# Output projections: the low halves of the scaled rows, subtracted by GpSimd behind each batch's bias instead of by VectorE

## The reference, cut to what matters

```python
    # layer 0: the heads are concatenated, no weight and no bias
    x = x + tanh(g_xattn[0]) * attention0(...)
    # layer 1 (and layer 6 in the same form)
    out = einsum('bhnm,bhmd->bhnd', softmax(scores), v).transpose(0, 2, 1, 3).reshape(b, n, c)
    x = x + tanh(g_xattn[1]) * (out @ Wproj + bproj)
    # layer 7: four quarters of the tokens, each with its own width m = 256, 128, 64, 32
    out = einsum('bnm,om->bno', attn_out[:, sl, :m], o_w[:m, :m]) + o_b[:m]
    x = x + tanh(g_ffn[3]) * (pad(out) + layernormed_x[:, sl, :])
```

## Time and profile before

| what | value |
|---|---|
| median of 3 runs | 6405.42 us (6404.94 to 6412.81) |
| the profiled execution: its own time | 6402.19 us |
| the profiled execution: its span | 6400.5 us |
| busy in the span | PE 4673.8 us (73%), DVE 3955.7 (62%), ACT 2808.6 (44%), POOL 2015.4 (31%) |
| granted TensorE clock, mean | 0.847 |
| the four output projections | 51 to 55 us each of the 6400.5 |

### The profile page before, as it was taken

The page is one execution under the profiler, slowest core; times in us unless marked ns, Lnnn a source line. Parts: engine busy times, 40 slices in busy tenths (PEclk is TensorE's granted clock), DMA queues, the critical chain, the costliest instruction groups (busy, mean ns, idle before and its releaser), DMA issues. The chain is left out here.

```text
span 6400.5 us, 101248 instructions
## 1 busy us (share of the span) xinstructions
PE 4673.8 (73%) x24710; PEld 2852.0 (45%) x24710; DVE 3955.7 (62%) x8261; ACT 2808.6 (44%) x5978; POOL 2015.4 (31%) x3020
## 2 busy tenths in 40 slices
PE   7455666482778972897675767797677887995897
PEld 4113333231453331786233645585555763334533
DVE  6335555547537875444477966558866556885465
ACT  2235554124225752322453556535466323771353
POOL 0114442000007640221353554124542214542242
PEclk9558999796898986998777979999889998996797
DMA  4999885000043320210551232102321115322433
GB/s 158 293 342 196 199 202 157 15 0 0 0 167 103 91 77 4 75 40 27 139 152 61 102 116 72 31 6 83 139 72 42 29 60 169 95 73 85 158 123 102
DMA packets 317804, 648.40 MB, mean 101 GB/s; under 512 B 73170, under 2 KB 128115, under 8 KB 317384
## 3 DMA queue, kind: packets, MB, share of 16 engines
q1 hardware_dynamic: 245912, 450.68, 21.8%
q0 software_dynamic: 71488, 193.32, 12.3%
HBM read 373.99 MB, written 238.70 MB: 96 GB/s over the span
## 5 line engine op out<-in xcount | busy, mean ns | idle before, releaser
L1115 DVE TENSOR_REDUCE t_nmax<-t_aps 128x2 f32<-128x1024 f32 x700 | 838.2, 1221 | 276.2 <-PE t_aps L1037 270.9
L1222 ACT ACTIVATE t_expT<-t_bps 128x512 f32<-128x512 f32 x1290 | 700.9, 599 | 283.8 <-PE t_bps L1056 233.4
L1056 PE MATMUL t_bps<-t_Q,t_K 51*128 51x512 f32 (+2 forms) x1290 | 525.9, 468 | 59.2 <-ACT t_expT L1222 43.4
L1037 PE MATMUL t_aps<-t_K,t_Q 49*128 49x512 f32 (+2 forms) x1400 | 464.6, 460 | 64.7 <-DMA t_K<-k_halves 30.0
L1056 PEld LDWEIGHTS t_bps<-t_Q,t_K 51*128 51x128 f32 (+2 forms) x1290 | 228.4, 189 | 526.2 <-ACT t_expT L1222 372.9
L2474 DVE TENSOR_TENSOR f_hl<-f_h,f_hh 128x512 fp32r<-128x512 f32 x192 | 203.7, 1061 | 411.2 <-ACT f_hh L2399 411.2
L1083 PE MATMUL t_ops<-t_expT,t_V 128*17 128x512 f32 (+1 forms) x2560 | 414.0, 615 | 0.4 <-ACT t_expT L1222 0.4
L3880 ACT ACTIVATE t_relsb<-t_relsb,t_nmax 128x128 f32<-128x128 f32 (+3 forms) x515 | 277.9, 559 | 272.1 <-DVE t_nmax L3853 268.7
L3814 PE MATMUL t_tps<-ident,t_relsb 128*128 128x128 f32 x1280 | 242.8, 292 | 165.5 <-ACT t_expT L3702 154.7
L2763 POOL TENSOR_TENSOR a_crossed<-a_qsb,a_tab 128x256 f32<-128x256 f32 x272 | 268.2, 1007 | 300.2 <-ACT a_qsb L2710 269.8
L1156 POOL DMA_DIRECT2D t_Q<-q_halves x525 | 270.9, 518 | 155.5 <-POOLq L78 86.2
(11 more groups left out here) (431 smaller groups left out, 12509.3 us busy)
## 6 DMA issues: line engine op xcount, KB each, us to landing
rel<-r_out SPq DMA_DIRECT2D x128, 640.0 KB, 5.4
t_relsb<-rel SPq DMA_DIRECT2D x128, 640.0 KB, 6.2
t_Q<-q_halves POOLq DMA_DIRECT2D x420, 64.0 KB, 2.5
t_K<-k_halves POOLq DMA_DIRECT2D x420, 64.0 KB, 2.6
k_halves<-a_parts SPq DMA_DIRECT2D x48, 512.0 KB
q_halves<-a_parts SPq DMA_DIRECT2D x48, 512.0 KB, 5.6
o_xT<-attended SPq DMA_DIRECT2D x32, 512.0 KB, 4.2
f_R<-combine SPq DMA_DIRECT2D x128, 128.0 KB, 2.9
```

What stands on the lines that cost most here:

```text
L1037: last = nc.tensor.matmul(aps[:, (t * PPG + i) % 2, x, :], operand(Qr, KA, p, h, slice(t * P, (t + 1) * P)), operand(Kr, KA, p, h, slice(0 ...
L1056: nc.tensor.matmul(bps[:, slot_of(kb, j), :], operand(Kr, KB, p, h, slice(kb * P, (kb + 1) * P)), operand(Qr, KB, p, h, slice(0, S)), star ...
L1115: nc.vector.tensor_reduce(nmax[:, g, t, i * HPT:(i + 1) * HPT], aps[:, (t * PPG + i) % 2], AX.X, ALU.max, negate=True).then_inc(s["maxed"], 1)
L1222: nc.scalar.activation(expT[:, kb % RING, j, :], bps[:, slot_of(kb, j), :], ACT.Exp).then_inc(s["expo"], 1 + (PAD if end else 0))
```

## The change

`lower(b)` moves from VectorE's program into GpSimd's. There it stands behind the bias of the same batch; in o0, which has no bias, the eight of them stand alone. What it computes and what it waits for (`xh` of its batch, and `y` of the batch two before, which frees the `xl` buffer) is unchanged.

```diff
+                def lower(b):
+                    pool.wait_ge(s["xh"], (b + 1) * KO)
+                    wait(pool, "y", (b - 1) * 2)
+                    nc.gpsimd.tensor_tensor(fast(xl[:, b % 2]), xn[:, b % 2], xh[:, b % 2], ALU.subtract).then_inc(s["xl"], 1)
+
                 if bias is None:
+                    for b in range(NB):
+                        lower(b)
                     return
...
                     last.then_inc(s["biased"], 1)
+                    lower(b)
...
-                def lower(b):
-                    dve.wait_ge(s["xh"], (b + 1) * KO)
-                    wait(dve, "y", (b - 1) * 2)
-                    nc.vector.tensor_tensor(fast(xl[:, b % 2]), xn[:, b % 2], xh[:, b % 2], ALU.subtract).then_inc(s["xl"], 1)
...
                 scale(0)
-                lower(0)
                 for b in range(NB):
                     if b + 1 < NB:
                         scale(b + 1)
                     if b:
                         add(b - 1)
-                    if b + 1 < NB:
-                        lower(b + 1)
                 add(NB - 1)
```

## The result

The changed kernel took 6413.27 us (median of 20 runs, 6391.84 to 6430.65), the kernel before, on the same chips, 6399.10 (20 runs, 6382.13 to 6413.23). The ratio is 1.0023, with a 95% interval from 1.0013 to 1.0034: slower by 14.2 us, and by 8 to 22 us with the interval, so whether it is more or less than 0.2% stays open. The profiled execution of the change took 6418.53 us, with a span of 6416.9.

The account below looks back on a forecast made before the run. VectorE sets the steady pace by a hair over TensorE, which waits on the line from spread to `xl`. The terms 1.7 + 2.4 + 4.6 + 4.1 = 12.8 us on the 6405.42 median gave 6418.2, range 6411 to 6432, the forecast's own 6415 to 6421.

Parts of the forecast that it names:

- The subtraction's price: All four output projections: one subtraction takes 2.36 us alone on GpSimd against 1.22 on VectorE, 1.14 more.
- o0: the line: o0: spread to project through GpSimd's subtraction takes 5.00 us, two batches at least 7.94; project(7) 1.7 us later.
- o1 and o3: GpSimd the bound: o1, o3: bias plus subtraction cost GpSimd 4.65 us a batch against TensorE's 3.59; +2.4 us and +4.6 us.
- aren't held up either: o1, o3: with both on GpSimd, neither its biases nor the subtraction are held up by the other engine.
- The clock rival: o1, o3, o0: TensorE's idling drops its clock from 2.4 to 1.2 GHz; 6428, or 6438 if throughout; chance 0.18.
- such a collision: First batches: a GpSimd bias holds up VectorE's subtraction, 3.44 us in place of 1.22 at 5799.29; mostly covered.
- my 10 us: Clock low in half of the twelve batches, 6 times 1.65 us, put on top of the forecast: 6428.
- The ring: o7: scale to `xh` 1.97, GpSimd's subtraction 2.36, then the held-up L1547 1.21: 5.54 us a batch.
- +4.1: o7: L1547 waits for nearly the whole GpSimd subtraction each batch; phase ends at 6389.4 against 6385.3, +4.1 us.
- The rival in which L1547 isn't held up: o7 keeps its time, the sum is 8.7 us, 6414; chance 0.11.
- The sum: All four phases: 1.7 + 2.4 + 4.6 + 4.1 = 12.8 us, with unknown lags 12 to 15.
- The relief of VectorE: Rival, not slower: VectorE's batch falls from 3.66 to 2.44 us, 0.4 gained per phase, 6403; chance 0.07 with similar outcomes.

Follow-up runs that it names:

- the repeated profiles: Both kernels run and profiled again, unedited: the change 6416.54 us against 6399.31, ratio 1.0024; the kernel before against itself 0.9994.
- Run 3: Changed kernel with GpSimd's subtraction in two halves, each begun once its half of `xh` is there; one execution, 6396.62 us.
- Run 2: Changed kernel with the bias of o1 and o3 left out, so GpSimd only subtracts there; one execution, 6417.01 us.
- Run 7: Kernel before, with the bias fetched earlier and o7's adds of `inner` for batches 3 to 7 made in the head; 6392.12 us, ratio 0.9992.
- run 4: Kernel before, VectorE's subtraction kept, plus a second copy on GpSimd that nobody reads and scale waits for; 6450.74 us in one run.
- run 6: Changed kernel with o7's add of `inner` (L1551) put ahead of the same batch's four other adds; 6411.20 us, ratio to before 1.0025.
- run 1: Changed kernel with o7's eight adds of `inner` (L1551) made ahead of the stretch in which GpSimd subtracts; one execution, 6427.33 us.

## Why the prediction was right, step by step

**The subtraction's price** held: 2.36 us forecast from one row of another phase, 2.36 in the median of 32.

**o0: the line.** Predicted was a pair of batches in 7.94 us and project(7) later by 1.7. TensorE's timeline of the change:

```profile
1118.34 0.73 PE L1451 MATMUL o_rps<-o_rows,o_sel 32*128 32x512 f32 x2
1118.99 0.39 PE L1461 MATMUL o_yps<-o_Wh,o_xh 128*128 128x256 f32 x1
...
1121.93 0.72 PE L1451 MATMUL o_rps<-o_rows,o_sel 32*128 32x512 f32 x2
...
1123.40 0.39 PE L1461 MATMUL o_yps<-o_Wh,o_xh 128*128 128x256 f32 x1 [0.74 <-POOL o_xl L1493]
```

From the start of a spread to the next project it is 0.65 in one batch, then 1.47, and starts of project are 4.41 and 3.61 apart, 8.02 a pair. The start of project(7) behind spread(2) was 24.8 us, against 22.78: +2.0 (+1.75 between the repeated profiles). Run 3 shortened the line and the pair with it.

**o1 and o3: GpSimd the bound.** Predicted 4.65 a batch. GpSimd's and TensorE's timelines in o1:

```profile
2404.04 2.37 POOL L1493 TENSOR_TENSOR o_xl<-o_xn,o_xh 128x1024 fp32r<-128x1024 f32 x1
2406.38 2.39 POOL L1511 TENSOR_TENSOR stream<-stream,o_B 128x1024 f32<-128x1024 f32 x1
2408.74 2.37 POOL L1493 TENSOR_TENSOR o_xl<-o_xn,o_xh 128x1024 fp32r<-128x1024 f32 x1
```

```profile
2411.16 0.39 PE L1461 MATMUL o_yps<-o_Wh,o_xh 128*128 128x256 f32 x1 [1.03 <-POOL o_xl L1493]
...
2415.85 0.38 PE L1461 MATMUL o_yps<-o_Wh,o_xh 128*128 128x256 f32 x1 [1.03 <-POOL o_xl L1493]
```

GpSimd is back to back, 4.70 from one subtraction to the next, TensorE idles 1.03 us and starts a project each 4.69. Project(7) behind spread(2): 28.69 against 25.84 in o1, +2.85 (+2.4 predicted, +2.4 in the second pair), and 28.54 against 23.84 in o3, +4.7 (+4.6 predicted, +4.9 in the second). Of the 0.45 that the prediction lacked in o1, about half lies ahead of project(2) and half in 4.69 a batch in place of 4.65. Run 2 took the bias away and the bound went. That GpSimd's biases "aren't held up either" held too: 2.339 to 2.399 us in all 16.

**The clock rival did not come.** Windows of TensorE in o1 of the change:

```profile
2412.00:2416.00 4.00, 2.97 (x23) 1.00 0.00 0
2420.00:2424.00 4.00, 3.00 (x24) 1.00 0.00 0
```

The engine idled 1.03 us of each 4.69 at a granted clock of 1.00, that is 2.4 GHz, from 3 us behind spread(2) to the last project, in o1 and in o3 and in both profiles of the change; even the 1.67 us before project(7) did not change it. The clock of the kernel before, in both of its profiles, fell once in o1 (0.61 in the earlier trace rows), and in the change this fall is gone: that is part of why o1 lost 2.85 and o3 4.7. Run 7 corrects the prediction here. It said that most of such a collision is covered, yet the one in o1 had cost 3.0 us with the fall of the clock behind it; the sum stands all the same, since it is taken from the measured start of project(7). The late fall in run 3 cost some 1.5 us, and with idles of 1.7 to 2.0 us in every batch (run 4) the clock fell again and again. So the rival is not excluded for another execution; where it came it cost less than my 10 us. The granted clock of the span, 0.844, doesn't tell: the phases are a thirtieth of it.

**o7: right mechanism, a term too large.** VectorE's and GpSimd's timelines in the change:

```profile
6366.06 1.09 DVE L1542 SCALAR_TENSOR_TENSOR stream<-o_yps,gate,stream 128x256 f32<-128x256 f32 x4
6367.18 3.12 DVE L1551 SCALAR_TENSOR_TENSOR stream<-inner,gate,stream 128x1024 f32<-128x1024 f32 x1
6370.22 1.27 DVE L1531 TENSOR_TENSOR o_xn<-o_xT,o_rps 128x512 f32<-128x512 f32 x2
```

```profile
6366.87 2.34 POOL L1493 TENSOR_TENSOR o_xl<-o_xn,o_xh 128x1024 fp32r<-128x1024 f32 x1 [0.77 <-ACT o_xh L1480]
...
6372.22 2.34 POOL L1493 TENSOR_TENSOR o_xl<-o_xn,o_xh 128x1024 fp32r<-128x1024 f32 x1 [0.43 <-ACT o_xh L1480]
```

GpSimd is first by 0.31 (0.35 predicted), L1551 stands until 6369.21, and the next scale follows 1.01 behind that, not 1.21. The ring is 2.00 + 2.34 + 1.01 = 5.35 us, where I had 5.54. It ran as predicted, five rounds from the subtraction of batch 2 to that of batch 7, 26.8 us where I had 27.7. The sixth hold-up, behind the last subtraction, left 5.72 us to the end in place of 5.94. So the mis-sized term is what an L1551 that was held up still needs once GpSimd is done: 1.01 us, not 1.21, six times. The bias did not stay at 1.63 either: behind L1551 it took 2.61, which still ended 0.43 before the next subtraction could start. By project(7) the phase lost 2.8 (29.3 to 32.08; 2.0 in the second pair), to its end 2.95 and 2.2: the "+4.1" was too large by 1.2 to 1.9. The rival in which L1547 isn't held up fell with the row of 3.12 and with run 6, in which order alone brought project(7) forward by 1.95 us. This is what the page SBUF — State Buffer of the Trainium skill, section "SBUF: two separate sides", states: of GpSimd and a VectorE instruction with two inputs in SBUF, whichever starts first holds their shared port pair for the whole instruction, and the other blocks. Here 3.12 us in place of 1.28 agrees.

**The sum.** Predicted 12.8; 2.0 + 2.85 + 4.7 + 2.95 = 12.5 us in the first profiles, 1.75 + 2.3 + 4.9 + 2.2 = 11.15 in the second, 14.2 between the medians of the runs. o7's excess and the small shortfalls of o0 and o1 nearly cancel. The relief of VectorE, 9.8 us of its time per phase (8 × 1.22), paid nowhere: no phase became shorter. The predicted time of 6418.2 stood on a median of 6405.42 from 3 runs; over 20 runs that median is 6399.1, and this alone moves it by 6. So the absolute time proves little: 6413.27 lies below the forecast's own 6415 to 6421 and next to the 6414 of the rival in which L1547 isn't held up. What bears the forecast out is the difference, 14.2 for 12.8, and the phases; that the difference of the medians came so near, with an interval of 8 to 22 us, is in part luck.

## What to carry to other kernels

Before a step is moved to an idle engine, follow its input to whoever waits for its output: the engine's share of busy time says nothing of it. Here 1.14 us more on that line cost 2 us in o0, and a full GpSimd (two instructions of 2.35 beside a pace of 3.66) cost 2.3 to 4.9 in o1 and o3. Then add up, on the receiving engine, what it already does per batch. And where VectorE has instructions with two operands in SBUF beside GpSimd, ask who starts first in each round: an order that puts VectorE's first saved 3.1 us (run 6), though GpSimd's bias then waited instead, where moving the same instructions into the head of the phase saved 4.7 in the steady part and lost 5.7 in the head (run 1).

## What I had not expected

- The one-operand cast from fp32 to fp32r on VectorE (128x32) also stood behind GpSimd: 1.29 us in place of 0.18 (run 1). VectorE's instructions that read PSUM did not, in the change: two of L1531, begun at 1122.56 while GpSimd subtracted since 1120.98, took 1.28, and two of L1545, begun at 2406.54 while GpSimd added a bias since 2406.38, took 1.41.
- A held-up instruction ends sooner after its release than one started then would: 1.01 us to the next instruction's start (o7), 1.21 where nothing held it up.
- TensorE kept 2.4 GHz with 1.03 us idle in every 4.69, and fell to 1.2 GHz before the change after an idle of 1.4 us, and in run 4 after idles of 1.7 us and more. Yet an idle of 1.67 us before project(7) of o3 in the change left it at 1.00, so the length of one idle alone doesn't tell. In o7 it was busy for 10.00 us of 10 at a granted clock of 0.50, before and after.
- Executions of one kernel wander by more than this change. The attention ahead of o0, the same code in all of them, took 573.1 us in the profile of before and 584.3 in its second one, 581.6 and 576.2 in the change's two; why it wanders is open. A single run with its 6396.62 (run 3) or 6427.33 (run 1) says nothing of 3 us; what is in a phase must be read in the phase.
